# A ternary feed-forward stage: biases added by the matmul accumulator, silu read from its bank, and a new order on ScalarE

## The reference, cut to what matters

```python
def bit_linear(x, w, b):
    gamma_x = clip(max(abs(x), axis=-1), 1e-05, None)
    scale_x = 127.0 / gamma_x
    x_dq = clip(round(x * scale_x), -128.0, 127.0) / scale_x
    gamma_w = clip(mean(abs(w)), 1e-05, None)
    w_dq = clip(round(w / gamma_w), -1.0, 1.0) * gamma_w
    return x_dq @ w_dq.T + b
gate = silu(bit_linear(x, gate_w, gate_b))      # 256 -> 1024
val = bit_linear(x, val_w, val_b)               # 256 -> 1024
return bit_linear(gate * val, out_w, out_b)     # 1024 -> 256
```

## Time and profile before

| | us |
|---|---|
| median of 3 runs (lowest, highest) | 2207.52 (2202.86, 2207.97) |
| profiled execution | 2204.45 |
| its span, first to last instruction | 2202.7 |

### The profile page before, as it was taken

One profiled execution on the slowest core, in us unless ns is written; L12 is line 12 of the kernel. 1 busy time (PEld: TensorE's weight loads), 2 busy tenths in 40 slices (PEclk: granted clock), 3 DMA queues, 4 the chain that ended last, 5 costly groups with the idle time before them and its releaser, 6 DMA issues. The chain is left out here.

```text
span 2202.7 us, 42217 instructions
## 1 busy us (share of the span) xinstructions
PE 1928.3 (88%) x11925; PEld 1297.9 (59%) x11926; DVE 1348.5 (61%) x3440; ACT 1065.7 (48%) x2793; POOL 717.3 (33%) x691
## 2 busy tenths in 40 slices
PE   7999999998999899979899989979967889888655
PEld 4666666665656566645676667635534557776433
DVE  6556556565777344446443434469969447777687
ACT  5545444553333222112344434357769437677575
POOL 3323333331000004443455556523200026666310
PEclk9999999999999889869999999989979989999787
DMA  9980000000000001143677777600010111111100
GB/s 310 279 223 0 0 0 0 0 1 1 0 0 0 1 1 61 61 162 104 146 160 173 163 164 127 125 1 2 1 60 1 65 36 34 30 40 31 31 17 22
DMA packets 145576, 145.11 MB, mean 66 GB/s; under 512 B 49376, under 2 KB 133568, under 8 KB 145344
## 3 DMA queue, kind: packets, MB, share of 16 engines
q1 hardware_dynamic: 122432, 113.81, 18.2%
q0 software_dynamic: 23040, 30.01, 7.9%
HBM read 137.12 MB, written 66.44 MB: 92 GB/s over the span
## 5 line engine op out<-in xcount | busy, mean ns | idle before, releaser
L1686 POOL DMA_INDIRECT expert_sums<-moe_rows_in,moe_to x128 | 197.9, 1546 | 158.0 <-DMA expert_sums<-moe_rows_in,moe_to 85.9
L1759 PE MATMUL moe_gate<-moe_places,moe_xt 128*128 x512 | 175.5, 465 | 3.1 <-issue 1.9
L1949 DVE COPY moe_ht_e<-moe_turned 128x256 f32<-128x256 f32 x128 | 54.3, 424 | 194.1 <-PE moe_turned L1767 194.1
L619 ACT ACTIVATE ga_prob<-ga_score,ga_neg_max 128x128 f32<-128x128 f32 x256 | 99.5, 390 | 145.7 <-DVE ga_neg_max L493 145.7
L240 POOL TENSOR_TENSOR ga_q_inv<-ga_q_sum,half 128x4 f32<-128x4 f32 x64 | 64.4, 1007 | 304.3 <-DVE ga_q_sum L476 304.3
L3017 POOL TENSOR_TENSOR wa_low<-wa_low,wa_top 128x512 f32<-128x512 f32 x128 | 133.0, 1039 | 89.8 <-DVE wa_top L3221 89.0
L2039 POOL TENSOR_TENSOR ln_rstd<-ln_var,half 128x4 f32<-128x4 f32 (+1 forms) x16 | 21.8, 1361 | 351.9 <-DVE ln_var L2035 351.8
L1153 POOL DMA_INDIRECT slot_x<-early x96 | 93.9, 979 | 112.0 <-DVE early L1144 73.3
L375 PE MATMUL ga_summed<-ga_wo,ga_out_t 128*128 128x256 f32 x512 | 122.5, 383 | 0.7 <-ACT ga_out_t L627 0.7
L375 PEld LDWEIGHTS ga_summed<-ga_wo,ga_out_t 128*128 128x128 f32 x512 | 98.1, 192 | 40.6 <-issue 29.2
L3218 DVE SCALAR_TENSOR_TENSOR wa_low<-wa_score,early 128x512 f32<-128x512 f32 x128 | 87.7, 685 | 55.0 <-PE wa_score L3057 52.5
(11 more groups left out here) (482 smaller groups left out, 4952.0 us busy)
## 6 DMA issues: line engine op xcount, KB each, us to landing
moe_places<-in_L_ffn_packed SPq DMA_DIRECT2D x128, 608.0 KB
slot_x<-zeros SPq DMA_DIRECT2D x24, 1076.0 KB, 16.1
moe_rows_in<-slot_x SPq DMA_DIRECT2D x128, 134.5 KB, 2.7
wa_v<-v_ctx SPq DMA_DIRECT2D x16, 180.0 KB, 3.1
early<-in_L_xattn_Wq SPq DMA_DIRECT2D x5, 512.0 KB, 7.8
x<-in_x SPq DMA_DIRECT2D x4, 512.0 KB, 9.2
ga_wo<-in_L_xattn_Wo SPq DMA_DIRECT2D x1, 2048.0 KB, 14.0
expert_sums<-zeros SPq DMA_DIRECT2D x2, 1024.0 KB, 8.2
```

The source lines that it names most:

```text
L619: last = act.activation(prob[:, n % 2, part], score[:, n % 2, part], ACT.Exp, bias=neg_max[:, n % 2, h:h + 1], accum_out=total[:, n % 2, h ...
L1686: pool.indirect_dma_start(out=mem.sums[j % SUMS], out_offset=bass.IndirectOffsetOnAxis(ap=to[:, j:j + 1], axis=0), in_=y[:, j, :], in_offs ...
L1759: last = pe.matmul(both[j % 2][:, 0:2 * FE], xt[:, j % 2, c, :], packed[:, place, c * 2 * FE:(c + 1) * 2 * FE].rearrange("p a n -> p (a n) ...
```

## The change

- The biases are divided by the mean of w once, in place (`bias_over_mean`, with `per_mean` from two reciprocals). For each tile DVE makes a diagonal matrix of the inverse of the tile's step (`spread_inverse`: 128x128 f32, two of them in turn). Each of the four halves of a tile's `up` gets a third matmul, diagonal by bias, both f32, accumulated into the same bank; so the bank times the scale holds the biased value.
- `pre`, `val` and the four DVE instructions of `before_silu` are gone. ACT's silu reads the gate's bank with the tile's scale and writes one of two `gate` arrays. DVE multiplies the value's bank by scale and gate in two `scalar_tensor_tensor` of 128x512 (in place of one 128x1024 product). A gate bank is thus free for PE behind the silu, a value bank behind the product.
- In ACT's loop `silu(n+1)` stands ahead of `round_product(n)`.
- The first half of every `up` waits also for its diagonal and its scaled bias; `finish(n-1)` follows `measure(n)` and the group's work directly.

The diff, cut to its core:

```diff
-        pre, gate, val, prod, shifted = (sb(x, [P, F]) for x in ("pre", "gate", "val", "prod", "shifted"))
+        gate = sb("gate", [P, 2, F])
+        prod, shifted = (sb(x, [P, F]) for x in ("prod", "shifted"))
+        diagonal, per_mean = sb("diagonal", [P, 2, P]), sb("per_mean", [P, 2])
...
+        diagonals, per_means, biases = signal("diagonals"), signal("per_means"), signal("biases")
+        silued, multiplied = signal("silued"), signal("multiplied")
...
-                def up(n, out_banks, weight, read, done):
+                def up(n, out_banks, weight, bias, j, read, done):
                     pe.wait_ge(rows_moved.sem, rows_moved.at(n // GROUP))
                     for h in range(2):
                         behind(pe, read, 2 * (n - 1) + h)
                         for c in range(HC):
-                            last = pe.matmul(out_banks[h][:, :], mem.xnt16[:, c, n * P:(n + 1) * P], weight[:, c, h * HALF:(h + 1) * HALF], start=(c == 0), stop=(c == HC - 1))
-                        last.then_inc(done.sem, 1)
+                            pe.matmul(out_banks[h][:, :], mem.xnt16[:, c, n * P:(n + 1) * P], weight[:, c, h * HALF:(h + 1) * HALF], start=(c == 0), stop=False)
+                        if h == 0:
+                            pe.wait_ge(diagonals.sem, diagonals.at(n))
+                            pe.wait_ge(biases.sem, biases.at(j))
+                        pe.matmul(out_banks[h][:, :], diagonal[:, n % 2, :], bias[:, h * HALF:(h + 1) * HALF], start=False, stop=True).then_inc(done.sem, 1)
...
+                        up(n + 1, gates, w.g, w.bg, 0, silued, gated)
+                        up(n + 1, vals, w.v, w.bv, 1, multiplied, valued)
...
                 def silu(n):
-                    behind(act, multiplied, n - 1)
+                    act.wait_ge(spread.sem, spread.at(2 * (n // GROUP)))
                     for h in range(2):
-                        act.wait_ge(pre_made.sem, pre_made.at(2 * n + h))
-                        act.activation(gate[:, h * HALF:(h + 1) * HALF], pre[:, h * HALF:(h + 1) * HALF], ACT.Silu).then_inc(silued.sem, 1)
+                        behind(act, multiplied, 2 * (n - 2) + h)
+                        act.wait_ge(gated.sem, gated.at(2 * n + h))
+                        act.activation(gate[:, n % 2, h * HALF:(h + 1) * HALF], gates[h][:, :], ACT.Silu, scale=scale_g[:, n:n + 1]).then_inc(silued.sem, 1)
...
-                    round_product(n)
                     if n + 1 < B:
                         silu(n + 1)
+                    round_product(n)
...
-                def halves(n, target, banks, scale, bias, made, done, read):
-                    dve.wait_ge(spread.sem, spread.at(2 * (n // GROUP) + 1))
-                    for h in range(2):
-                        cols = slice(h * HALF, (h + 1) * HALF)
-                        dve.wait_ge(made.sem, made.at(2 * n + h))
-                        behind(dve, *read(n, h))
-                        dve.scalar_tensor_tensor(target[:, cols], banks[h][:, :], scale[:, n:n + 1], bias[:, cols], ALU.mult, ALU.add).then_inc(done.sem, 1)
-
-                def before_silu(n):
-                    halves(n, pre, gates, scale_g, w.bg, gated, pre_made, lambda n, h: (silued, 2 * (n - 1) + h))
-                    halves(n, val, vals, scale_v, w.bv, valued, val_made, lambda n, h: (multiplied, n - 1))
+                def spread_inverse(n):
+                    if n % GROUP == 0:
+                        dve.wait_ge(norm.scaled.sem, norm.scaled.at(n // GROUP))
+                    behind(dve, valued, 2 * (n - 2) + 1)
+                    dve.tensor_scalar(diagonal[:, n % 2, :], mem.ident[:, :], norm.scale[:, n:n + 1], None, ALU.mult).then_inc(diagonals.sem, 1)
+
+                def bias_over_mean(j, bias):
+                    dve.wait_ge(per_means.sem, per_means.at(j))
+                    dve.tensor_scalar(bias[:, :], bias[:, :], per_mean[:, j:j + 1], None, ALU.mult).then_inc(biases.sem, 1)
...
-                    dve.wait_ge(silued.sem, silued.at(2 * n + 1))
-                    dve.wait_ge(val_made.sem, val_made.at(2 * n + 1))
+                    dve.wait_ge(spread.sem, spread.at(2 * (n // GROUP) + 1))
                     behind(dve, lifted, n - 1)
-                    dve.tensor_tensor(prod[:, :], val[:, :], gate[:, :], ALU.mult).then_inc(multiplied.sem, 1)
-                    dve.wait_ge(multiplied.sem, multiplied.at(n))
+                    for h in range(2):
+                        dve.wait_ge(valued.sem, valued.at(2 * n + h))
+                        dve.wait_ge(silued.sem, silued.at(2 * n + h))
+                        dve.scalar_tensor_tensor(prod[:, h * HALF:(h + 1) * HALF], vals[h][:, :], scale_v[:, n:n + 1], gate[:, n % 2, h * HALF:(h + 1) * HALF],
+                                                 ALU.mult, ALU.mult).then_inc(multiplied.sem, 1)
+                    dve.wait_ge(multiplied.sem, multiplied.at(2 * n + 1))
...
+                spread_inverse(0)
+                for j, mean_of in enumerate((w.mean_g, w.mean_v)):
+                    dve.reciprocal(per_mean[:, j:j + 1], mean_of[:, 0:1]).then_inc(per_means.sem, 1)
+                bias_over_mean(0, w.bg)
                 norm.variance(dve, LASTG * GROUP, B)
                 norm.shifts(dve, 1, LASTG * GROUP, B)
                 dve.wait_ge(mem.tf_loaded.sem, 16 * 3)
-                before_silu(0)
+                bias_over_mean(1, w.bv)
                 for n in range(B):
                     g, k = divmod(n, GROUP)
+                    if n + 1 < B:
+                        spread_inverse(n + 1)
...
-                    if n + 1 < B:
-                        before_silu(n + 1)
```

More of the change, by code:

```diff
@@ L3406, in ternary_ffn @@
         gated, valued = signal("gated"), signal("valued")
-        pre_made, val_made, silued, multiplied = signal("pre"), signal("val"), signal("silued"), signal("multiplied")
+        diagonals, per_means, biases = signal("diagonals"), signal("per_means"), signal("biases")
+        silued, multiplied = signal("silued"), signal("multiplied")
         chain, per_made = signal("chain"), signal("per")
@@ L3459, in _ @@
                 turn_rows(0)
-                up(0, gates, w.g, pre_made, gated)
-                up(0, vals, w.v, val_made, valued)
+                up(0, gates, w.g, w.bg, 0, silued, gated)
+                up(0, vals, w.v, w.bv, 1, multiplied, valued)
                 for n in range(B):
                     if n + 1 < B:
-                        up(n + 1, gates, w.g, pre_made, gated)
-                        up(n + 1, vals, w.v, val_made, valued)
+                        up(n + 1, gates, w.g, w.bg, 0, silued, gated)
+                        up(n + 1, vals, w.v, w.bv, 1, multiplied, valued)
                     if n % GROUP == 2 and n // GROUP < LASTG:
```

## The result

The median of four runs is 2252.82 us (2242.19 to 2257.23), against 2207.74 for four runs of the kernel before (2202.86 to 2213.69): a ratio of 1.0197, with a 95% interval of 1.0162 to 1.0232. The kernel is slower by 2.0%, 1.6 to 2.3. The profiled execution took 2242.19 us, its span 2240.3, against 2204.45 and 2202.7.

The account below looks back on a forecast made before the run. DVE bounded the kernel at 6.44 us a tile. First `shifted` at 2086.06, 14 cycles of 8.55, three times 4.5 + 2.0, and 4.35 give 2229.6; net 36 us on 2204.45 makes 2240 us, range 2226 to 2258.

Parts of the forecast that it names:

- The f32 product: PE's added bias matmuls: each f32 product is two records and costs 0.86 us, so an `up` grows from 0.87 to 2.59.
- The cycle: Settled tiles: each tile goes once around PE and ACT in series, 8.55 us in place of DVE's 6.44.
- its mean of 7.28 us: Last stage before the change: 109.27 us for 15 tiles; every third tile of a group stops ACT at `move_rows`.
- The third tile: Third tile of a group: `move_rows` ahead of silu waits for transposes behind both `up`s, 4.5 us extra, three times.
- The cold stretch behind it: After the third tile's pause PE runs `go_down`, gates and transposes at 1.2 GHz: 2.0 us each, bounds 0 and 3.5.
- The start: Start of the stage: cold gates from 2075.47, first `shifted` at 2086.06 in place of 2083.25.
- The end: Tile 15, without `up` or silu ahead, takes 4.35 us; from the last `shifted` on, about 1.2 us less than before.
- The prediction's own sum: Whole stage: last `shifted` at 2229.6 against 2192.52, 37.1 us later, less 1.2 at the end: 36 us.
- The clock held in settled tiles: Rival: PE stays at 1.2 GHz in settled tiles, 5.5 us more each; four give 2262, all 2310; chance 0.12.
- The f32 products cost what the rows at L743 said: Rival: f32 against a diagonal runs in one pass, each `up` 1.29 us shorter, 2215 us; chance 0.12.
- PE's stream was in order: Rival: PE gets gates in ahead of the wait for `move`, its 6.6 us a tile sets pace, 2197; chance 0.04.
- No price on the path in settled tiles: DVE's added diagonal, bounded by 0 and 0.744 us, is off the path; DVE falls to about 4.2 us a tile.

## Why the prediction was right

It said 2240 us, from a profiled execution of 2204.45, and that execution's counterpart took 2242.19. The mechanism is the one that it named, a tile's work in series around PE and ACT. That the number came so near is in part luck: the traced execution was the fastest of four, and one error was hidden by another (below). Laid on the median of the kernel before, the forecast 36 us give 2244, where the median is 2253; 36 us is 1.6%, the lower edge of the measured interval. Step by step:

- **The f32 product.** Two records of 592 ns each, 0.43 us apart: an `up` takes 2.58 us (2213.68 to 2216.26) against 2.59. The 128 records that the prediction named for the gates were a slip in its last part: 16 tiles x 2 halves are 32 products, so 64 records, which is what L3441 shows; the sum had counted four per `up`, rightly.
- **The cycle.** 8.57 us against 8.55. The order without the circle, and the circle opened by the gates ahead, give 7.77, PE's own series. That it needs the silu to read its bank was not said in the prediction, but I believed it until the order alone was tried in the kernel before; the cause is ACT's order together with PE's place for the gates.
- **The kernel before.** The prediction put its mean of 7.28 us, over 6.44, down to the third tiles. They hold 6.8 of the 12.7 us above 15 x 6.44; the intervals that follow the first tile of a group (7.63, 7.84 and 7.84 us) hold 4.0. In the changed kernel these are 8.51, 8.57 and 8.57, so this second cause was hidden under the cycle and the sum didn't miss it.
- **The third tile.** 13.0 us, 4.45 above the cycle, against 4.5:

```profile
2186.22 0.61 PE L3448 MATMUL tf_turned_in<-ident,tf_out_of 128*128 128x128 bf16 x8
...
2186.86 1.02 ACT L3500 ACTIVATE tf_xnt<-tf_turned_in 128x1024 bf16<-128x1024 bf16 x1 [6.75 <-PE tf_turned_in L3448]
...
2187.78 1.26 ACT L3484 ACTIVATE tf_gate<-tf_gates,tf_scale_g 128x512 f32<-128x512 f32 x2
...
2188.92 1.25 ACT L3488 ACTIVATE tf_shifted<-tf_prod,tf_up_by,tf_per 128x1024 f32<-128x1024 f32 x1
...
2191.47 1.03 PE L3455 MATMUL tf_turned<-ident,tf_rounded 128*128 128x128 bf16 x8 [4.64 <-ACT tf_rounded L3491]
...
2193.61 1.89 PE L3462 MATMUL tf_down<-tf_o,tf_ht 128*128 128x256 bf16 x8 [1.12 <-ACT tf_ht L3496]
...
2195.30 1.06 PE L3437 MATMUL tf_gates<-tf_g,tf_xnt 128*128 128x512 bf16 x2
...
2199.96 1.23 ACT L3488 ACTIVATE tf_shifted<-tf_prod,tf_up_by,tf_per 128x1024 f32<-128x1024 f32 x1
```

The rows' transposes stand behind the values (2186.22), `move_rows` behind them, both silus and `shifted` (2188.92) behind that, and PE has nothing for 4.64 us.

- **The cold stretch behind it.** Mis-sized: I took 2.0 us each, the tile from 2188.92 to 2199.96 is 11.04, so 2.5 above the cycle, and 2.8 and 2.7 the other two times; 1.9 us in all were missing. `go_down` took 1.69 to the gates, as taken; more of the gates' f32 products ran at 1.2 GHz than I had allowed.
- **The start.** First `shifted` 10.87 us behind the first gates; I had 10.59.
- **The end.** Wrong by 1.2 us. I expected the last transposes and `go_down` at full clock; they took 1.03 and 1.89 us, as before. Between the end of the last values (2227.6) and 2232.62, PE had only the transposes and `go_down` of tile 14, 0.62 and 1.05 us.
- The prediction's own sum is thus short by 3.5 us, of which 1.9 was taken back by a stage that began earlier.
- **The rivals.** The clock held in settled tiles (1.00 in the window from 2160), except behind third tiles. The f32 products cost what the rows at L743 said, 0.86 us each (0.43 for each of two records) and not half of it, and PE's stream was in order.
- **DVE.** No price on the path in settled tiles, as said: the diagonal takes 0.28 us (the median of 16) and DVE waits 62.6 us for `shifted` in all.

The Trainium skill's 131 ns for a matmul of 512 columns ("TensorE: Matmul & The Clock Gate", section "Back-to-back issue gap"), weighed in the prediction, isn't what this trace shows: the pace is 0.22 us in bf16 (two from 2213.68 to 2214.11) and 0.43 for an f32 record.

What stays open: the median of four runs is 2252.82, 10.6 us above the profiled execution, whereas before it was 3. The other three runs have spans of 2246.4 to 2255.3 at granted clocks of 0.944 to 0.947, against 0.950, so PE was at 1.2 GHz for longer in them; in which stage isn't known, since there is a timeline of one only. The range of 2221 to 2262 held them.

## What to carry to other kernels

Before moving an instruction ahead of another in one engine's stream, walk from it through every engine's order back to itself: here silu ahead of the rounding put two engines' work in series, and cost 41 us alone in the trace (32 by the ratio), about half of it by the lower clock that came with it. Moving work from the bounding engine to one with idle time pays only if that idle time isn't a wait inside the same loop; PE's added work cost about 30 us, and DVE's relief gave at most 5.5 back. If a circle closes, try to issue the work it waits for one tile earlier before giving the order up. Here that alone wasn't enough (0.4% slower than before); only with PE's and ACT's streams both reordered was the same change, f32 biases and all, faster than the kernel before, by 0.5%.

## What was not expected of the hardware

Less work for PE lowered its clock enough to give back a third of the gain: bf16 biases took a pause from 0.63 to 1.9 us a tile and the granted clock over the stage from 0.90 to 0.82, and the stage gained 17 us where 26 were worked out at full clock. It isn't so whenever PE has less to do: with both streams reordered the bf16 biases gained 21 us, at a granted clock of 0.90 against 0.94 with f32.

The same kernel before took 2206 us on one chip and 2230 on another, 1.1% apart. Most of this seems to lie ahead of the stage that is studied here: there is no trace of the kernel before on either, but in the traces of its variants the first gates start at 2076 to 2083 us in one session and at 2100 to 2108 in the other's.
